# A four-layer fused transformer kernel: five of 24 row-maximum units move behind the slot boundary, and the maxima are placed in two halves

## The reference

```python
k = layernorm8(x @ Wk); q = layernorm8(x @ Wq); v = x @ Wv   # 16 heads of 8 channels
q, k = q * 128 ** -0.25, k * 128 ** -0.25
dot = einsum('bihd,bjhd->bhij', q, k)
dot = where(j > i, -inf, dot)
att = softmax(dot, axis=-1)
x1  = layernorm(x + (einsum('bhij,bjhd->bihd', att, v) @ Wo + bo))
```

## Time and profile before

| what | value |
|---|---|
| timed runs | 1452.73, 1458.58, 1454.91 us, median 1454.91 |
| the profiled execution's own time | 1459.59 us |
| its span | 1457.9 us, 18213 instructions |
| mean granted TensorE clock | 0.839 of full |
| PE busy | 1148.9 us, 79% |
| DVE busy | 964.5 us, 66% |
| ACT busy | 618.6 us, 42% |
| POOL busy | 446.1 us, 31% |

### The profile page before, as it was taken

The page is one execution under the profiler, slowest core; times in us unless marked ns, Lnnn a source line. Parts: engine busy times, 40 slices in busy tenths (PEclk is TensorE's granted clock), DMA queues, the critical chain, the costliest instruction groups (busy, mean ns, idle before and its releaser), DMA issues.

```text
span 1457.9 us, 18213 instructions
## 1 busy us (share of the span) xinstructions
PE 1148.9 (79%) x5332; PEld 583.4 (40%) x5332; DVE 964.5 (66%) x2391; ACT 618.6 (42%) x1170; POOL 446.1 (31%) x460
## 2 busy tenths in 40 slices
PE   2778888998999988999897602049898898988997
PEld 1323345553555535545355302014344343443443
DVE  3616536556477676866667668888888898888221
ACT  1061551835618447184374202025444463444542
POOL 3031220302334043331350451253443534435210
PEclk7566797897988989889799856569898998989898
DMA  4111030120313204133013373101022020210000
GB/s 103 65 45 58 9 102 9 44 88 31 102 40 95 87 31 132 38 88 96 23 32 84 83 215 77 46 7 46 8 53 61 8 53 8 53 29 0 22 7 8
DMA packets 85336, 79.83 MB, mean 55 GB/s; under 512 B 42769, under 2 KB 62865, under 8 KB 83217
## 3 DMA queue, kind: packets, MB, share of 16 engines
q1 hardware_dynamic: 85264, 79.01, 19.6%
HBM read 43.45 MB, written 35.00 MB: 54 GB/s over the span
## 4 chain that ended last, share of the span: by engine, by line
PE 60%; DVE 18%; ACT 8%; issue 8%; POOL 2%; SPq 1%; DMA 1%; ACTq 0%; DVEq 0%; POOLq 0%
PE ps L1195 14%; PE ps L1181 9%; PE ps L871 6%; PE ps L933 5%; PE ps L903 4%; DVE arena L1689 4%; ACT arena L1335 3%; PE ps L922 3%; PE ps L906 3%; ACT arena L1297 2%; PE ps L1187 2%; PE ps L962 2%; PE ps L982 2%; PE ps L992 2%; PE ps L1000 2%
## 5 line engine op out<-in xcount | busy, mean ns | idle before, releaser
L1297 ACT ACTIVATE arena<-ps 128x512 f32<-128x512 f32 (+2 forms) x200 | 110.3, 572 | 337.6 <-PE ps L871 214.7
L1689 DVE TENSOR_REDUCE arena<-ps 128x2 f32<-128x1024 f32 (+3 forms) x176 | 194.9, 1124 | 56.3 <-PE ps L906 53.4
L1195 PE MATMUL ps<-arena,late 128*128 128x512 f32 x512 | 225.6, 592 | 0.0
L1335 ACT ACTIVATE arena<-ps 128x1024 f32<-128x1024 f32 (+3 forms) x256 | 169.9, 718 | 33.7 <-PE ps L922 32.1
L721 POOL TENSOR_SCALAR_AFFINE_SELECT arena<-arena 128x512 f32<-128x512 f32 x128 | 84.4, 662 | 304.1 <-ACT arena L1335 303.1
L871 PE MATMUL ps<-ident,arena 128*128 128x128 f32 (+1 forms) x640 | 115.3, 328 | 40.8 <-ACT arena L1297 12.2
L1181 PE MATMUL ps<-arena,late 128*128 128x512 f32 x256 | 135.2, 689 | 12.4 <-ACT arena L1470 12.4
L1195 PEld LDWEIGHTS ps<-arena,late 128*128 128x128 f32 x512 | 96.2, 190 | 115.8 <-issue 115.5
L903 PE MATMUL ps<-kr,qr 32*128 32x512 f32 (+3 forms) x512 | 107.7, 470 | 35.6 <-issue 20.5
L1470 ACT ACTIVATE arena<-ps,f_s 128x512 f32<-128x512 f32 x128 | 87.2, 688 | 70.3 <-PE ps L1195 46.4
L871 PEld LDWEIGHTS ps<-ident,arena 128*128 128x128 f32 (+1 forms) x640 | 83.5, 161 | 81.8 <-issue 23.4
(11 more groups left out here) (164 smaller groups left out, 1964.6 us busy)
## 6 DMA issues: line engine op xcount, KB each, us to landing
scan_d<-late SPq DMA_DIRECT2D x64, 138.0 KB, 3.0
qr<-q_rep SPq DMA_DIRECT2D x8, 1024.0 KB, 5.8
kr<-k_rep SPq DMA_DIRECT2D x8, 1024.0 KB, 8.0
arena<-scan_d SPq DMA_DIRECT2D x12, 552.0 KB, 6.8
q_rep<-hilo SPq DMA_DIRECT2D x24, 256.0 KB, 3.1
k_rep<-hilo SPq DMA_DIRECT2D x24, 256.0 KB, 3.8
proj_d<-arena SPq DMA_DIRECT2D x8, 768.0 KB, 5.1
late<-proj_d SPq DMA_DIRECT2D x8, 768.0 KB, 4.5
```

What stands on the lines that cost most here:

```text
L1195: last = pe.matmul(ps[:, ring2.bank(f"{n}{c}"), :], w[:, k, c * P:(c + 1) * P], src[:, k, :], start=(k == 0), stop=(k == HC - 1))
L1297: return act.activation(dst, src(ps[:, bank, :]), func, **kw)
L1335: act.activation(prob[:, gg % 2, 2 * pr:2 * pr + 2, p_off[jt]:p_off[jt] + w], ps[:, bank:bank + 2, 0:w], ACT.Exp).then_inc(p_taken, 1)
L1689: v.tensor_reduce(heads[:, 2 * pr:2 * pr + 2, gs[0]:gs[-1] + 1], ps[:, 2 * (k % 2):2 * (k % 2) + 2, 0:len(gs) * w].rearrange("p q (n w) -> ...
```

## The change

The 22 units become 24, ordered by halves of the heads: twelve for groups 0 and 1, then twelve for groups 2 and 3. Each half has two units for `it` 0 (two groups each, 256 columns per bank), two for `it` 1, four for `it` 2 and four for `it` 3. Units 0 to 18 stay at the end of the slot before; units 19 to 23 (one for `it` 2, four for `it` 3) stand in the next slot, one before the third token logits and one in each of the first four steps of the scores. Maxima and scores now draw their pairs of banks from one ring (`pairs`). The maxima are turned, copied and placed by halves: the first half after unit 13 (two DMAs), the second half in the next slot at (gg, jt) = (1, 1), with a wait for it before group 2. On DVE `take_combined` goes ahead of units 16 to 18. POOL's `add_bias` waits for y1 instead of xr. ACT ends each slot with an exponential of one column into a spare tile.

The parts of the diff below are, in order: the constants, the tiles and rings, SP, POOL, PE, ACT and DVE.

```diff
+X_LATE = 19
+NM_AT, XR_AT = 13, 14
...
-        nm_T = c1.take(S)[0:NH, :]
+        nm_T = [c1.take(S)[0:NH // 2, :], x2T[0:NH // 2, :]]
...
+        K = Handoff(k_ready, {"dve": k_dve}, [], [("nm1", "dve")])
...
-                                (T, "L3"), (T, "M0"), (T, "M1"), (T, "M2"), (T, "M3"), (T, "cT0"), (T, "cT1"),
+                                (T, "L3"), (T, "M0"), (T, "M1"), (T, "M2"), (T, "M3"), (K, "nm1"), (T, "cT0"), (T, "cT1"),
...
-                                (G, "c0"), (G, "c1"), (G, "c2"), (G, "c3"), (T, "pr"), (T, "mo"), (N1, "x1T"), (F, "nmT")])
+                                (G, "c0"), (G, "c1"), (G, "c2"), (G, "c3"), (T, "pr"), (T, "mo"), (F, "nm0"), (N1, "x1T")])
...
-        for it in range(NT):
-            per = {0: 4, 1: 2}.get(it, 1)
-            for g0 in range(0, NG, per):
-                for pr in range(2):
-                    x_units.append((it, pr, list(range(g0, g0 + per))))
+        for h in range(2):
+            for it in range(NT):
+                per = 2 if it < 2 else 1
+                for g0 in range(2 * h, 2 * h + 2, per):
+                    for pr in range(2):
+                        x_units.append((it, pr, list(range(g0, g0 + per))))
...
+        XL = Handoff(s_ready, {"dve": s_taken}, [], [(f"x{k}", "dve") for k in range(NX)])
+        XE = Handoff(s_ready, {"dve": s_taken}, [], [(f"e{k}", "dve") for k in range(NX)])
+        AS = Handoff(p_ready, {"act": p_taken}, [], [(f"s{k}", "act") for k in range(len(p_units))])
+        seq = [(XE, f"e{X_LATE}")]
+        for at in range(len(p_units) // 2):
+            seq += [(AS, f"s{2 * at}"), (AS, f"s{2 * at + 1}")]
+            if X_LATE + 1 + at < NX:
+                seq.append((XE, f"e{X_LATE + 1 + at}"))
+        seq += [(XL, f"x{k}") for k in range(X_LATE)]
+        pairs = Ring([0, 2], seq)
...
+            def turn(b, kept, tail, x):
+                place_maxima(b, 1)
+                if kept is not None:
+                    store_heads(kept)
+                replicate(b + 1)
+                if tail is not None:
+                    store(tail)
+                place_maxima(b + 1, 0)
+                if x is not None:
+                    load_x(x)
+                if tail is not None:
+                    load_heads(tail)
...
-                g.wait_ge(xr_ready, CREDIT + b)
+                if not first:
+                    g.wait_ge(n_dve, CREDIT + N1.emptied("ao", b - 1))
...
                 if pre is not None:
+                    if i is not None:
+                        g.wait_ge(xr_ready, CREDIT + i + 1)
                     scale_heads(pre)
...
                 if moe is not None: 
-                    for t in range(3):
-                        token_logits(moe, turn, t)
+                    token_logits(moe, turn, 0)
+                    token_logits(moe, turn, 1)
+                early()
+                if moe is not None:
+                    token_logits(moe, turn, 2)
                 if b is not None:
-                    pe.wait_ge(max_placed, CREDIT + (b + 1) * 64)
+                    pe.wait_ge(max_placed[0], CREDIT + (b + 1) * 32)
...
-                            scores(b, gg, jt)
+                            if (gg, jt) == (2, 0):
+                                pe.wait_ge(max_placed[1], CREDIT + (b + 1) * 32)
+                            scores(b, gg, jt, turn)
+                        if front is not None and (gg, jt) in ((0, 0), (0, 1)):
+                            project_qkv(front, turn, 2 * jt)
+                        if moe is not None and (gg, jt) == (0, 2):
+                            token_logits(moe, turn, 3)
+                        if moe is not None and (gg, jt) == (0, 3):
+                            slot_logits(moe, turn, 1)
+                        if gg == 0:
+                            early()
...
+                        if b is not None and (gg, jt) == (1, 1):
+                            transpose_maxima(b, turn, 1)
...
-                maxima_to(X1 + 2)
+                if front is not None:
+                    transpose_maxima(front, turn, 0)
+                maxima_to(X_LATE - 3)
                 if b is not None:
                     transpose_x1(b, turn)
-                if front is not None:
-                    maxima_to(NX)
-                    transpose_maxima(front, turn)
+                maxima_to(X_LATE)
...
                 if b is not None:
                     take_x1(b)
+                    act.activation(warm[:, :], ident[:, 0:1], ACT.Exp)
...
                 apply(o, xr, y1, s, s[:, 5, :]).then_inc(xr_ready, 1)
-                reduce_to(NX)
+                reduce_to(X_LATE - 3)
+                if moe is not None and front is not None:
+                    take_combined(moe)
+                reduce_to(X_LATE)
...
+                def rest():
+                    if moe is not None:
+                        yield top(moe, "M", 1)
+                    yield early()
+                    if moe is not None:
+                        yield top(moe, "M", 2)
+                        yield top(moe, "M", 3)
                 if moe is not None:
-                    for t in range(3):
-                        top(moe, "L", t)
+                    top(moe, "L", 0)
+                    top(moe, "L", 1)
+                early()
+                if moe is not None:
+                    top(moe, "L", 2)
...
-                        advance(o_fold, folds, 4)
+                        advance(o_fold, folds, 2)
+                early()
+                if moe is not None and folded is not None:
+                    advance(o_fold, folds, 2)
+                early()
+                if moe is not None:
                     top(moe, "L", 3)
+                early()
+                if moe is not None:
                     top(moe, "M", 0)
-                    tops = slot_tops(moe)
+                tops = rest()
                 if front is not None:
-                    norms(front, (lambda: next(tops, None)) if tops else None)
+                    norms(front, lambda: next(tops, None))
+                for _ in tops:
+                    pass
+                if b is not None:
+                    take_maxima(b, 1)
```

More of the change, by code:

```diff
@@ L910, in transpose_maxima @@
-            def transpose_maxima(b, turn):
-                pe.wait_ge(s_taken, CREDIT + (b + 1) * NX)
-                transposes("nmT", turn, [neg_max[:, t, :] for t in range(NT)]).then_inc(f_ready, 1)
-            def scores(b, gg, jt):
+                it, pr, gs = x_units[k]
+                pairs.wait_free(pe, use, *turn)
+                at = pairs.bank(use)
+                w = (it + 1) * P
+                banks = [ps[:, at + n, 0:len(gs) * w].rearrange("p (n w) -> p n w", w=w) for n in range(2)]
@@ new lines, in scores_for_maxima @@
+                for j, gg in enumerate(gs):
+                    for n, bank in enumerate(banks):
+                        q = 2 * pr + n
+                        rows = slice(32 * q, 32 * q + 32)
+                        pe.matmul(bank[:, j, :], qr[rows, gg, it * P:(it + 1) * P], kr[rows, gg, 0:w],
+                                  start=(j == 0), stop=False)
+                for bank in banks:
+                    last = pe.matmul(bank[:, :, it * P:w], ident_b[:, :],
+                                     mask_qk[:, :].unsqueeze(1).broadcast_to([P, len(gs), P]), start=False, stop=True)
@@ L916, in scores, with transpose_maxima @@
+                last.then_inc(s_ready, 1)
+            def transpose_maxima(b, turn, h):
+                pe.wait_ge(s_taken, CREDIT + b * NX + (h + 1) * (NX // 2))
+                transposes(f"nm{h}", turn, [neg_max[:, t, 8 * h:8 * h + 8] for t in range(NT)]) \
+                    .then_inc((f_ready, k_ready)[h], 1)
+            def scores(b, gg, jt, turn):
                 for k in range(gg * PU + 2 * jt, gg * PU + 2 * jt + 2):
                     _, _, pr = p_units[k]
-                    pe.wait_ge(p_taken, CREDIT + b * len(p_units) + max(k - 1, 0))
+                    pairs.wait_free(pe, f"s{k}", *turn)
@@ L1025, in slot, with early @@
             def slot(b, moe, front, tail, before):
-                now = {h: i for h, i in ((N1, b), (T, moe), (F, front), (G, tail)) if i is not None}
+                now = {h: i for h, i in ((N1, b), (K, b), (XE, b), (AS, b), (T, moe), (F, front), (XL, front), (G, tail))
+                       if i is not None}
                 turn = (now, before)
+                early_at = X_LATE
+                def early():
+                    nonlocal early_at
+                    if b is not None:
+                        scores_for_maxima(b, f"e{early_at}", turn)
+                    early_at += 1
                 if front is not None:
@@ L1141, in _ @@
             pe.wait_ge(slot_taken, 1)
-            scores_for_maxima(0, 0, NX)
-            transpose_maxima(0, first)
+            for k in range(X_LATE):
+                scores_for_maxima(0, f"x{k}", first)
+                if k == NM_AT:
```

(1 more changed line is left out.)

160 lines of the change are left out of this document (66 added, 94 removed).

## The result

The change did not make the kernel faster. In the same session the kernel after takes a median of 1458.95 us (1455.45 to 1461.9, 19 runs) and the kernel before 1453.75 us (1450.2 to 1458.58, 19 runs): ratio 1.0031, interval 1.0020 to 1.0042, 0.3% slower. That is 5.2 us, within the 0.5% that the prediction called no change, where 1439 us and faster had been forecast. Measured again, it is 1458.21 against 1454.52 us, ratio 1.0017 (1.0003 to 1.0030).

What follows compares the result with a forecast made beforehand. PE held 60% of the chain, so gains lay where DVE or hand-overs separate its work. Slots 1 to 6 give 9.6 us, slot 7 3.3, slot 0 2.9: 15.8 off 1459.6, 1443.8; by the median 1439, range 1417 to 1464.

Steps and rivals of the forecast that it cites:

- What has cover: Side effects across a slot (nm1's placing, group 2's wait, norms, `load_x`, POOL's scaling): taken as 0, between -1 and +1 us per slot.
- xr then follows x12: At a slot's end: DVE starts xr behind unit x12, at about 511.7 instead of 515.34, and needs 1.1 us.
- 5.7 - 4.1 = 1.6 us: Each of slots 1 to 6: 5.7 us won at the boundary, 4.1 lost from s0 to s8; 9.6 us in six slots.
- The boundary: From a slot's last x units to the next s0: s0 comes 5.7 us earlier, the middle of two clock cases.
- The bounds of 3.7 and 7.7: How much earlier s0 comes at the boundary: 3.7 us at the low clock throughout, 7.7 at the high clock.
- The shared port: Rival, `take_combined` held for a whole POOL operation: 1.3 us instead of 0.2, six slots lose 6.6; 1446 us; chance 0.05.
- s0 to s8: First scores, with four late units between them: M2's top and s8 come 4.1 us later, bounds 1.5 and 8.5.
- e22: Late unit between the first scores, behind L3's top on DVE: 0.7 us of PE, 1.2 of DVE; s7 waits for it.
- rivals of the boundary: Clock stays up over the boundary: 1425 us, chance 0.24. Clock stays down until after s0: 1453 us, chance 0.15.
- 7.6 - 4.7 + 5.7: Slot 0 up to the next s0: 7.6 us won by its s0, 4.7 lost among its scores, 5.7 won at the boundary.
- What I had said would show it: Signs of being right: PE's pause only x16 to x18; s0 5 to 8 us earlier; no table load before L0; slot near 90.5.
- signs of being wrong: s0 to s8 near 19 or 12.5 us; boundary clock 1.0 or 0.50 throughout; PE idle before L871; waiting for maxima at group 2.

Runs made afterwards that it cites:

- e12_all_four: The change without slot 7's new POOL wait, with `XR_AT` 13, halves added behind x18 and eight extra matmuls between score steps: 1443.09 us, ratio 0.9902 to the kernel before.
- e4_e23_after_m2: The change with the last late unit, e23, behind M2's top on DVE instead of ahead of it: 1476.57 us, ratio 1.0133 to the kernel before.

## Why the prediction was wrong

**The direction.** Forecast was a gain of 15.8 us, measured is a loss of 5.2. The 21 us between them are two steps and the clock. That 1458.95 lies between the stated 1417 and 1464 is luck: the upper end stood there for a low clock over the whole boundary, and not for a wait in slot 7.

**The first step that failed** is in "What has cover": "POOL scales the heads some 4 us earlier [...] I take 0 for all of this". I looked at the boundary of a full slot, where the new wait for xr only writes out the old order, and did not ask where the wait stands without an old one. That is slot 7: 8.5 us, shown from both sides, taken out of the change and put alone into the kernel before. The rows of before had it: POOL began at 754.36, before y1, with DVE's folds directly behind xr.

**The second** is "xr then follows x12". In the diff `XR_AT` is 14, with nm0's copy after unit 13, so xr follows x13 and the copy. I took xr at y1 + 19.3; it was at y1 + 21.5, and with `XR_AT` 13 it is 19.6. With this one line as I had read it the change takes 1446.27 us, and with slot 7 mended too 1437.46, where 1439 was forecast. The forecast was close for a kernel that was not the one in the diff, and even there in part by luck (18.1 us gained where 15.8 was forecast). For a full slot of that kernel the sum has 5.7 - 4.1 = 1.6 us; measured are 5.7 from C and D, 4.9 lost in A and 1.7 won in B, 2.5 together, and the 1.7 (1.1 against the other execution of the same slots) was counted at nothing.

**The boundary.** For it I had 5.7 us. In the changed kernel C and D together gave 4.5 (40.8 to 36.3); in the mended one 5.7 (35.1). Against the same kernel without late units, D fell by 5.5 there. The bounds of 3.7 and 7.7 held both.

**The shared port.** I took 0.2 us and gave the rival 0.05; the add took 1.83 us instead of 0.69, and PE waited 2.68 us in front of x18. That is 1.1 us in such a slot, and on the length of the add the rival was right in the change. It did so in slots 3 to 6 only: slots 1 and 2 have no heads to scale, so four slots and not six. The 0.84 us that I took as the plain time was already beside POOL's L752; alone it is 0.69 (248.64 and 340.87 in the trace of before). The Trainium skill (SBUF — State Buffer, SBUF: two separate sides) has it that whichever of such two operations starts first holds the pair of ports for its whole length. By that rule the 0.05 us by which POOL began first (504.42 against 504.47) decide, and the trace agrees both ways: with DVE first by 0.07 us it is POOL's operation that grows, to 1.74 us. Taking this microsecond off the boundary did not change the time in either run that tried it: with the add behind x18 D stayed as it was, and with POOL's scaling freed D shrank, but C grew by more.

**s0 to s8.** At the full clock A is 15.1 us, a loss of 4.2; forecast 4.1. The working, tops and late units one after another on DVE behind L3, was right. In the mended kernel, from s0 at 600.58, DVE reaches L3's top 7.8 us after s0 (5.8 before: 2.1 late, forecast 1.8), goes on without a pause through e22, the norms' reduction and e23, and comes to M2's top:

```profile
608.40 0.69 DVE L1758 TENSOR_REDUCE arena<-ps 128x1 f32<-128x512 f32 x1 [1.53 <-PE ps L974]
...
614.37 0.68 DVE L1758 TENSOR_REDUCE arena<-ps 128x1 f32<-128x512 f32 x1
```

What was not in the sum is that the low clock can fall into A: at 0.81 it is 17.7. In the change it did so in four slots.

**The clock.** I had it as rivals of the boundary alone, with the gain between 3.7 and 7.7, and of the groups behind I said "PE's clock in the groups after may fall at other places", between -1 and +1. Here the size was wrong. Before, the clock in the 12 us behind s8 was 0.63 to 0.66 in four slots of six and 0.86 in one (in the other execution, 0.64 to 0.65 in three and 1.00 in three); after, it is 1.00 in all, and B is 1.7 us shorter (1.1 by the other execution). Part of this low clock came back in A. I had bounded by 1 us what moved by 2 in both directions. The Trainium skill (TensorE: Matmul & The Clock Gate, HAM oscillation) says that PE's pauses between bursts bring the low clock back each time round. In D the trace of the change agrees in every full slot (0.75 to 0.77); in one slot of `e12_all_four` D ran at 1.00 nevertheless and took 11.9 us, where that run's others took 14.5 to 15.6. What decided here is whether the next fall came in A or in B, and no run shows a rule for that.

**Slots 0 and 7.** At slot 0's s0 the change is 10.1 us ahead (69.81 against 79.95; forecast 7.6). At the next s0, where the sum has 8.6 (7.6 - 4.7 + 5.7), it is 12.9 ahead in one pair of executions (148.88 against 161.78) and 6.5 in the other (151.89 against 158.43), so that slot 0 alone scatters by more than most terms of the sum. Slot 7's A lost 4.5 us (15.93 against 11.46; forecast 2.4).

**What I had said would show it.** No table load before L0: right (it ends at 504.2). PE's pause shrinks to x16 to x18: right. s0 to s8 15 us: only at full clock. A full slot near 90.5: it was 91.7, and 89.8 in the mended kernel. Of the signs of being wrong, one showed faintly: PE waited for the placed maxima ahead of group 2 in slots 1 and 2, 0.6 us together, where I had seen 5 us of slack.

**Not settled.** Why 2 us in the place of xr lets the clock stay up between s0 and s8, and why e23 one place later brings it down behind s8; in the second case there is at least a new pause of PE, 1.63 us in front of s9, but it stands in slot 2 as well, where the clock stayed up. With the added matmuls the clock in A stayed up in five slots of six; nothing here shows what the chip would do for a given order, and runs of one kernel differ in it (1432.88 to 1443.75 us with both mends).

## What to carry to other kernels

When a wait is moved from one operation to another, go through every call of both, the first and the last round of a pipeline above all: where the old operation is not called, the wait is new. Read the constants of a diff against the loop that uses them before timing anything by them (a unit `k` that is taken "up to 14" includes 13). And where a change shortens the pauses of PE, sum the stages at an equal clock first, then give each long stretch behind the change a bound of its own for the low clock, of the size that it has in the rows of before.

## What the runs showed that I had not expected

- A two-input DVE step of 128x4 beside a POOL operation of 128x512 takes 1.25 to 1.30 us instead of 0.15: beside POOL the shortest steps lose the most for their length. Freeing POOL earlier can cost more than it brings.
- The three folds in slot 7, beside POOL's four products, took 2.72 us instead of 1.09, and the products 3.87 instead of 3.33.
- Moving one reduction of 1.2 us by one place in DVE's order cost 18 us (`e4_e23_after_m2`), while s8 itself came earlier: a new pause of PE in front of s9 and, for the larger part, the clock.
- Five late units are worth 10.5 us or nothing, by the place of one other operation.
